# Seven block products in place of eight for the gate and up projections of sixteen experts in one decoder layer

## Chip, cores and metric

One core of a Trainium2 chip runs the whole layer as one program. The metric is the device time of one execution in microseconds (us); lower is better. The engines are PE (TensorE), DVE (VectorE), ACT (ScalarE), POOL (GpSimd) and SP (SyncE, which here only issues transfers). Each engine runs its own instruction list in order and waits on semaphores.

## What is computed

x is 8 x 512 tokens of width 512. Two attention parts add to it; then comes the feed-forward part, which the change touches:

```python
N, NK, C = 4096, 8192, 640                      # C = CAP: slots of an expert
probs = softmax(h @ router_w + router_b)        # h: normed tokens, 16 experts, top 2
expert_inputs[idx, pos] = h[token]              # (16, 640, 512)
y = (silu(e @ w_gate) * (e @ w_up)) @ w_down    # per expert, F = 704
out = x + shared_mlp(h) + sum over k of y[idx, pos] * weight
```

All inputs and outputs are fp32. A product of two fp32 matrices is made of three TensorE passes: each operand is split into a high part (rounded to fp32r by a copy) and a low part (the word minus its high part), and high*high, high*low and low*high are added in PSUM.

## The kernel before

Phase 1 (attention, router) runs batch by batch. Phase 2 has 24 groups: groups 0 to 7 are the shared MLP on the 8 batches of 512 tokens, groups 8 to 23 are the 16 experts, each on 640 gathered tokens (ET = 5 tiles of 128 tokens). F = 704 is cut into FC = 6 chunks of 128, the last of 64.

The weights of one job (shared, or one expert) are WC = 17 chunks of 128x512: gate and up for chunks 0 to 4 (ten), one "mixed" chunk with the last 64 columns of gate and of up, and six of down. Each goes from HBM to one of RAW = 6 raw buffers (SP, `load_weights`), then ACT copies its high part into a ring of 22 slots and POOL subtracts to get its low part (`split` on both engines, POOL's is L1426).

For one expert PE runs, for each of the five full chunks and each half of the tokens (`cuts`: 2 x 320 columns), gate and then up: four K chunks by three passes, so 5 x 2 x 2 x 12 = 240 matmuls of 320 columns, and 2 x 12 more for the mixed chunk (all in `three_pass`, L72). ACT makes silu of the gate (L1533), DVE multiplies it by up (L1599) into PSUM, ACT rounds the product (`h_hi`, L1491), DVE subtracts (`h_lo`, L1583). Then come the down products: five token tiles of 17 matmuls with 512 columns (L1692), which alternate between two PSUM banks. PE may start tile t only when DVE has scaled tile t-2 out of its bank:

```python
if n >= 2:
    pe.wait_ge(s_ost, n - 1)
```

Beside the down tiles the next expert's tokens are made ready. POOL has gathered them (L1439) at the start of this group, SP has turned them with DMA transposes into two 16-bit planes, ACT writes the upper halves of the words (`x_top`) and DVE the lower ones (`x_low`, L1567); ACT rounds (`x_hi`), DVE subtracts (`x_lo`, L1573). `tail` sets the order: work for token tile t, then the scaling of down tile t (L1636), which POOL adds to the output with an indirect DMA (L1480). L1491 is the line of the helper `copy`, so all ACT copies of phase 2 have it.

## Time and profile before

| what | value |
|---|---|
| time, median of 3 runs | 1820.36 us (1820.07 to 1820.89) |
| span of the profiled execution | 1818.3 us |
| PE busy | 1804.8 us, 99% |
| DVE, ACT, POOL busy | 873.3, 800.0, 922.2 us |
| one expert, start to start | 58.0 us |

The profiled execution's span is its own time as far as the profile shows it; it lies 2.1 us below the median of the runs. The kernel has 16 experts of equal work from 880.6 us to the end; the window of a whole expert taken below is 1112.58 to 1170.59 us, its gate and up until 1151.29 and its down tiles from there.

### The profile page before, as it was taken

To read this page: it belongs to the slowest core of one execution; us is meant where nothing else is said; L and a number is where in the kernel's file an instruction comes from. 1 tells how busy PE (TensorE), PEld (TensorE's weight loads), DVE (VectorE), ACT (ScalarE), POOL (GpSimd) and SP (SyncE) were. 2 spreads that over 40 slices of the span, in tenths; PEclk is the share of its full clock that TensorE was granted. 3 is DMA by queue.
4 is the path that set the end of the run, shared out by engine and by line. 5 is a ranking of instruction groups with operands and counts; after the bars stand their busy time and mean duration, and the time that the engine had idled before them with its cause. 6 is when DMAs were issued, how large, how long until landed. Compare 5 with 4: busy or idle time off the path is not lost.

```text
span 1818.3 us, 27202 instructions
## 1 busy us (share of the span) xinstructions
PE 1804.8 (99%) x9977; PEld 1598.7 (88%) x9977; DVE 873.3 (48%) x2067; ACT 800.0 (44%) x1574; POOL 922.2 (51%) x809
## 2 busy tenths in 40 slices
PE   9999999999999999999999999999999999999997
PEld 6888888888887878888999999999999999999997
DVE  6668777787745444332444324343334423443242
ACT  4555556555544343332444434444344434444331
POOL 3454464546653232225665656556665566656632
PEclk9999999999999999999999999999999999999999
DMA  8454555453552333225676676666666766667722
GB/s 319 147 134 122 151 140 150 134 143 95 147 116 40 47 52 68 37 42 103 161 141 132 163 156 134 135 150 158 147 140 126 164 149 140 145 138 163 145 41 29
DMA packets 254436, 229.35 MB, mean 126 GB/s; under 512 B 171712, under 2 KB 171968, under 8 KB 253024
## 3 DMA queue, kind: packets, MB, share of 16 engines
q1 hardware_dynamic: 228864, 174.51, 36.7%
q0 software_dynamic: 25440, 53.11, 17.3%
q8 instruction: 79, 1.29, 0.3%
q14 instruction: 53, 0.43, 0.1%
HBM read 138.80 MB, written 49.97 MB: 104 GB/s over the span
## 4 chain that ended last, share of the span: by engine, by line
PE 94%; DVE 2%; DMA 1%; issue 1%; POOL 1%; ACT 1%; SPq 0%; POOLq 0%; DVEq 0%; ACTq 0%
PE ps L72 66%; PE ps L1692 23%; PE ps L1002 3%; PE ps L1146 1%; PE ps L1008 0%; DMA buffer<-means 0%; ACT buffer L528 0%; DMA buffer<-in_x 0%; POOL buffer L481 0%; DMA means<-mean 0%; DVE buffer L832 0%; DVE stats L736 0%; DMA tokens_normed<-buffer 0%; ACT buffer L1491 0%; DMA buffer<-buffer 0%
## 5 line engine op out<-in xcount | busy, mean ns | idle before, releaser
L72 PE MATMUL ps<-buffer,buffer 128*128 128x320 f32 (+1 forms) x6900 | 1239.1, 341 | 1.3 <-DVE buffer L832 0.8
L72 PEld LDWEIGHTS ps<-buffer,buffer 128*128 128x128 f32 x6900 | 1121.0, 188 | 107.5 <-issue 1.5
L1426 POOL TENSOR_TENSOR buffer<-buffer,buffer 128x512 fp32r<-128x512 f32 x289 | 380.4, 1480 | 251.6 <-ACT buffer L1491 251.1
L1692 PE MATMUL ps<-buffer,buffer 128*128 128x512 f32 (+1 forms) x1921 | 437.6, 388 | 0.4 <-DVE buffer L1624 0.4
L1692 PEld LDWEIGHTS ps<-buffer,buffer 128*128 128x128 f32 x1921 | 356.9, 188 | 73.9 <-issue 1.2
L1533 ACT ACTIVATE buffer<-ps 128x320 f32<-128x320 f32 (+1 forms) x240 | 112.5, 469 | 599.6 <-PE ps L72 594.0
L1491 ACT ACTIVATE buffer<-buffer 128x512 fp32r<-128x512 f32 (+1 forms) x491 | 293.4, 652 | 163.4 <-PE ps L1692 90.6
L1599 DVE TENSOR_TENSOR ps<-ps,buffer 128x320 f32<-128x320 f32 (+2 forms) x198 | 100.2, 506 | 487.5 <-ACT buffer L1533 477.0
L1480 POOL DMA_INDIRECT out_tokens<-buffer,slot_list x79 | 124.0, 1569 | 185.5 <-DVE buffer L1636 177.3
L520 POOL DMA_INDIRECT slots<-pairs,slot_u x64 | 63.6, 994 | 181.8 <-DVE slot_u L989 164.8
L528 ACT ACTIVATE buffer<-buffer 128x512 fp32r<-128x512 f32 (+1 forms) x212 | 127.0, 683 | 19.9 <-DMA buffer<-buffer 15.2
L1636 DVE TENSOR_SCALAR buffer<-ps,slot_list 128x512 f32<-128x512 f32 (+1 forms) x81 | 60.1, 742 | 114.3 <-PE ps L1692 114.3
L533 ACT ACTIVATE buffer<-buffer,shift,rstd 128x512 f32<-128x512 f32 x96 | 70.5, 807 | 94.8 <-DVE shift L754 94.8
L1583 DVE TENSOR_TENSOR buffer<-ps,buffer 128x320 fp32r<-128x320 f32 (+2 forms) x198 | 96.7, 489 | 10.0 <-ACT buffer L1491 8.9
L1439 POOL DMA_INDIRECT buffer<-tokens_normed,slot_list x80 | 83.8, 1047 | 27.8 <-issue 27.8
L511 POOL TENSOR_TENSOR buffer<-buffer,buffer 128x512 f32<-128x512 f32 x32 | 40.5, 1293 | 103.1 <-DVE shift L754 99.1
L1491 ACT ACTIVATE buffer<-ps 128x320 fp32r<-128x320 f32 (+2 forms) x198 | 86.3, 436 | 0.7 <-DVE ps L1599 0.7
L528 ACT ACTIVATE buffer<-ps 128x512 fp32r<-128x512 f32 (+2 forms) x124 | 64.1, 557 | 43.9 <-PE ps L72 33.6
L1599 DVE TENSOR_TENSOR buffer<-ps,buffer 128x512 f32<-128x512 f32 (+1 forms) x42 | 29.0, 690 | 98.0 <-ACT buffer L1533 93.8
L1567 DVE COPY buffer<-buffer 128x512 uint16<-128x512 uint16 x80 | 72.0, 922 | 0.5
L736 DVE BATCH_NORM_STATS2 stats<-buffer 128x6 f32<-128x512 f32 x96 | 61.1, 682 | 7.8 <-DMA buffer<-in_x 7.7
L470 POOL TENSOR_TENSOR buffer<-buffer,buffer 128x512 fp32r<-128x512 f32 x28 | 38.4, 1405 | 37.3 <-ACT buffer L528 37.3
(134 smaller groups left out, 1094.0 us busy)
## 6 DMA issues: line engine op xcount, KB each, us to landing
buffer<-in_wts SPq DMA_DIRECT2D x289, 256.0 KB
buffer<-in_xT SPq DMA_DIRECT2D x8, 1024.0 KB, 5.5
buffer<-in_ctxT SPq DMA_DIRECT2D x8, 1024.0 KB, 8.2
out_tokens<-buffer SPq DMA_DIRECT2D x8, 1024.0 KB, 4.3
tokens_normed<-buffer SPq DMA_DIRECT2D x32, 256.0 KB, 3.1
out_tokens<-buffer POOLq DMA_DIRECT2D x32, 256.0 KB, 5.1
buffer<-in_x SPq DMA_DIRECT2D x7, 1024.0 KB, 5.5
buffer<-combiners_top SPq DMA_DIRECT2D x6, 1024.0 KB, 4.9
```

What stands on the lines that cost most here:

```text
L72: last = pe.matmul(out, left, right, start=(c == 0 and i == 0), stop=(c == len(parts) - 1 and i == 2))
L528: return act.activation(dst, src, ACT.Copy)
L533: act.activation(dst[:, t, :], x[b % XS][:, t, :], ACT.Identity, bias=shift[k][:, t:t + 1], scale=rstd[k][:, t:t + 1]).then_inc(done, 1)
L1426: pool.tensor_tensor(wl[n % RING][:], wraw[n % RAW][:], wh[n % RING][:].bitcast(F32), ALU.subtract).then_inc(s_wl, 1)
L1439: pool.indirect_dma_start(xn[:, t, :], None, Y[:, :], rows_at(groups[g][1], t), bounds_check=N + PAD - 1).then_inc(s_xg, 16)
L1480: pool.indirect_dma_start(out.rearrange("n (h d) -> (n h) d", h=parts), rows, ost[:, t, part_cols], None, bounds_check=parts * (N + PAD) - ...
L1491: return act.activation(dst, src, ACT.Copy)
L1533: act.activation(silu[u % TMP][0:rows_of(c), 0:n], bank[0:rows_of(c), 0:n], ACT.Silu)\
L1567: dve.tensor_copy(halves_of(t)[:, :, :, 0], xp[t][:, NC:2 * NC, :]).then_inc(s_xlow, 1)
L1583: dve.tensor_tensor(lo[:, first:first + n], product_of(u)[0:rows, 0:n], hh[0:rows, c, first:first + n].bitcast(F32), ALU.subtract).then_in ...
L1599: dve.tensor_tensor(product_of(u)[0:rows_of(c), 0:n], up_bank[u % 2][rows, 0:n], silu[u % TMP][0:rows_of(c), 0:n], ALU.mult).then_inc(s_ht, 1)
L1692: ins = pe.matmul(down_bank[(n + i) % 2][:, part_cols], left, right, start=(c == 0 and k == 0), stop=(c == FC - 1 and k == len(passes) - 1))
```

## The change

For experts only. A pair is the gate chunk and the up chunk of the same 128 features. Seen as a 2 x 2 block product (rows: gate and up; inner: two halves of K = 512; columns: two halves of the tokens, 64 of each tile of 128), it was eight block products. It becomes seven, by Winograd's form of Strassen's algorithm: three blocks of the weights and four sums of blocks (s1 to s4), against three blocks of the tokens and four sums of them (t1 to t4). A block product is 2 K chunks x 3 passes of 320 columns. The sums are made in fp32 on DVE and then split in high and low parts like all else (four slots for pairs, eight for single chunks; the ring is now the shared job's alone). The results need adding up after the product: two ACT copies out of PSUM (`kept`, `up1`) and five DVE additions (`pair_combined`); silu of the second half runs in SBUF. The high parts, sums and low parts of pair and single chunks are made at fixed places (`prepared`). POOL makes the low parts of all pairs in three instructions each (512, 256 and 1024 elements) and of four single chunks; DVE makes the other three (`BY_POOL = 4`). Both halves of the token words are now written by ACT. The gathered tokens (`xn`) share their place with `ost`.

The diff is cut to its core; plain renames and unchanged logic of the shared groups are left out.

```diff
-    RING = 22
     RAW = 6
     TMP = 3
-    TURN_AT = RAW + 4
+    PAIRS = FC - 1
+    SINGLES = WC - 2 * PAIRS
+    PAIR_SLOTS, SINGLE_SLOTS = 4, 8
+    PER_PAIR = 7
+    BY_POOL = 4
+    HALF, TH = CAP // 2, P // 2
+    TOKEN_PARTS = [(0, 2), (2, 4), (4, 5)]
...
+    prepared = {(3, 1): [("pair", 0)], (B - 1, 2): [("pair", 1)], (B - 1, 4): [("pair", 2)], (B - 1, "down0"): [("pair", 3)]}
+    for e in range(E):
+        q, m = e * PAIRS, e * SINGLES
+        prepared[B + e, 1] = [("pair", q + 4)]
+        prepared[B + e, 2] = [("single", m + i) for i in range(4)]
+        prepared[B + e, 3] = [("single", m + i) for i in range(4, SINGLES)]
+        if e + 1 < E:
+            prepared[B + e, 4] = [("pair", q + PAIRS)]
+            prepared[B + e, 5] = [("pair", q + PAIRS + 1)]
+            prepared[B + e, "down1"] = [("pair", q + PAIRS + 2)]
+            prepared[B + e, "down3"] = [("pair", q + PAIRS + 3)]
...
+        def low_parts(kind, i):
+            if kind == "single":
+                if i % SINGLES >= BY_POOL:
+                    return
+                n, k = single_chunk(i), single_slot(i)
+                pool.wait_ge(s_hi, parts_before_single(i) + 1)
+                pool.tensor_tensor(single_lo[k][:], wraw[n % RAW][:], single_hi[k][:].bitcast(F32),
+                                   ALU.subtract).then_inc(s_lo, 1)
+                return
+            n, k, done = pair_chunk(i), pair_slot(i), parts_before_pair(i)
+            hi, lo = pair_hi[k], pair_lo[k]
+            pool.wait_ge(s_hi, done + 1)
+            pool.tensor_tensor(lo[:, 0:2].rearrange("p b c f -> p (b c f)"), wraw[n % RAW][:],
+                               hi[:, 0:2].bitcast(F32).rearrange("p b c f -> p (b c f)"), ALU.subtract).then_inc(s_lo, 1)
+            pool.wait_ge(s_hi, done + 2)
+            pool.tensor_tensor(lo[:, 2].rearrange("p c f -> p (c f)"), wraw[(n + 1) % RAW][:, D // 2:D],
+                               hi[:, 2].bitcast(F32).rearrange("p c f -> p (c f)"), ALU.subtract).then_inc(s_lo, 1)
+            pool.wait_ge(s_hi, done + 3)
+            pool.tensor_tensor(lo[:, 3:7].rearrange("p b c f -> p (b c f)"),
+                               pair_sum[k][:].rearrange("p b c f -> p (b c f)"),
+                               hi[:, 3:7].bitcast(F32).rearrange("p b c f -> p (b c f)"), ALU.subtract).then_inc(s_lo, 1)
...
+        def high_parts(kind, i):
+            if kind == "single":
+                n = single_chunk(i)
+                loaded(act, n)
+                single_slot_free(act, i)
+                copy(single_hi[single_slot(i)][:], wraw[n % RAW][:]).then_inc(s_hi, 1)
+                return
+            n, hi = pair_chunk(i), pair_hi[pair_slot(i)]
+            loaded(act, n)
+            pair_slot_free(act, i)
+            copy(hi[:, 0:2].rearrange("p b c f -> p (b c f)"), wraw[n % RAW][:]).then_inc(s_hi, 1)
+            loaded(act, n + 1)
+            copy(hi[:, 2].rearrange("p c f -> p (c f)"), wraw[(n + 1) % RAW][:, D // 2:D]).then_inc(s_hi, 1)
+        def high_sums(kind, i):
+            if kind == "pair":
+                k = pair_slot(i)
+                act.wait_ge(s_sum, 4 * (i + 1))
+                copy(pair_hi[k][:, 3:7].rearrange("p b c f -> p (b c f)"),
+                     pair_sum[k][:].rearrange("p b c f -> p (b c f)")).then_inc(s_hi, 1)
+        def prepare(g, place, first=True, second=True):
+            for kind, i in prepared.get((g, place), []):
+                if first:
+                    high_parts(kind, i)
+                if second:
+                    high_sums(kind, i)
...
+        def words(e, t):
+            if t == 0:
+                act.wait_ge(s_xp, 16 * ET * (e + 1))
+                words_free(act, e)
+            copy(word_halves_of(t)[:, :, :, :, 1], turned_words(t, slice(0, NC))).then_inc(s_xraw, 1)
+            copy(word_halves_of(t)[:, :, :, :, 0], turned_words(t, slice(NC, 2 * NC))).then_inc(s_xraw, 1)
+        def token_hi(e, part):
+            cols = token_columns(part)
+            act.wait_ge(s_xraw, 2 * (ET * e + TOKEN_PARTS[part][1]))
+            if part == 0:
+                tokens_free(act, e)
+            copy(xh[:, :, :, cols], xw[:, :, :, cols]).then_inc(s_xh, 1)
+        def token_sum_hi(e, part):
+            n = len(TOKEN_PARTS) * e + part
+            cols = token_columns(part)
+            act.wait_ge(s_tsum, 4 * (n + 1))
+            act.wait_ge(s_xl, n + 1)
+            copy(th[:, :, :, cols], tw[:, :, :, cols]).then_inc(s_th, 1)
...
+        def pair_products(e, p):
+            g, q = B + e, e * PAIRS + p
+            u = unit_no[(g, p, 0)]
+            act.wait_ge(s_prod, PER_PAIR * q + 1)
+            if q > 0:
+                act.wait_ge(s_comb, 5 * (q - 1) + 2)
+            copy(kept[:], ps[0][:, 0:HALF]).then_inc(s_keep, 1)
+            if p > 0:
+                h_hi(e, p - 1, 0)
+                h_hi(e, p - 1, 1)
+            act.wait_ge(s_prod, PER_PAIR * q + 2)
+            if u - SHARED_UNITS >= 4:
+                act.wait_ge(s_hl, u - 2)
+            copy(up1[p % 2][:], cross_bank[p % 2][0][:, 0:HALF]).then_inc(s_keep, 1)
+            prepare(g, p, second=False)
+            act.wait_ge(s_prod, PER_PAIR * q + 4)
+            if q > 0:
+                act.wait_ge(s_ht, u - 1)
+            act.activation(silu0[:], ps[0][:, 0:HALF], ACT.Silu).then_inc(s_silu, 1)
+            prepare(g, p, first=False)
+            act.wait_ge(s_comb, 5 * q + 4)
+            act.activation(gate1[:], gate1[:], ACT.Silu).then_inc(s_silu, 1)
...
+            c = FC - 1
+            h_hi(e, c - 1, 0)
+            h_hi(e, c - 1, 1)
+            if e + 1 < E:
+                words(e + 1, 0)
+            for j, place in enumerate((silu0, gate1)):
+                act.wait_ge(s_mix, 2 * e + j + 1)
+                act.wait_ge(s_ht, unit_no[(g, c - 1, j)] + 1)
+                act.activation(place[0:FH, :], cross_bank[c % 2][j][0:FH, 0:HALF], ACT.Silu).then_inc(s_silu, 1)
+            for j in range(2):
+                h_hi(e, c, j)
+            prepare(g, c)
+            if e + 1 < E:
+                words(e + 1, 1)
+                token_hi(e + 1, 0)
+                words(e + 1, 2)
+                words(e + 1, 3)
+                token_hi(e + 1, 1)
+                token_sum_hi(e + 1, 0)
+                prepare(g, "down1")
+                words(e + 1, 4)
+                token_hi(e + 1, 2)
+                token_sum_hi(e + 1, 1)
+                token_sum_hi(e + 1, 2)
+                prepare(g, "down3")
...
+        def weight_sums(kind, i):
+            if kind == "single":
+                if i % SINGLES >= BY_POOL:
+                    n, k = single_chunk(i), single_slot(i)
+                    dve.wait_ge(s_hi, parts_before_single(i) + 1)
+                    dve.tensor_tensor(single_lo[k][:], wraw[n % RAW][:], single_hi[k][:].bitcast(F32),
+                                      ALU.subtract).then_inc(s_lo_dve, 1)
+                return
+            n = pair_chunk(i)
+            gate, up, sums = wraw[n % RAW], wraw[(n + 1) % RAW], pair_sum[pair_slot(i)]
+            s1, s2, s3, s4 = (sums[:, k].rearrange("p c f -> p (c f)") for k in range(4))
+            half = D // 2
+            loaded(dve, n)
+            loaded(dve, n + 1)
+            pair_slot_free(dve, i)
+            dve.tensor_tensor(s3, gate[:, 0:half], up[:, 0:half], ALU.subtract).then_inc(s_sum, 1)
+            dve.tensor_tensor(s1, up[:, 0:half], up[:, half:D], ALU.add).then_inc(s_sum, 1)
+            dve.wait_ge(s_sum, 4 * i + 1)
+            dve.tensor_tensor(s2, up[:, half:D], s3, ALU.subtract).then_inc(s_sum, 1)
+            dve.wait_ge(s_sum, 4 * i + 3)
+            dve.tensor_tensor(s4, gate[:, half:D], s2, ALU.subtract).then_inc(s_sum, 1)
...
+        def token_sums(e, part):
+            n = len(TOKEN_PARTS) * e + part
+            cols = token_columns(part)
+            b11, b21, b12, b22 = (xw[:, j, c:c + 2, cols] for j in range(2) for c in (0, 2))
+            t1, t2, t3, t4 = (tw[:, k, :, cols] for k in range(4))
+            dve.wait_ge(s_xraw, 2 * (ET * e + TOKEN_PARTS[part][1]))
+            if part == 0:
+                words_free(dve, e)
+            dve.tensor_tensor(t1, b12, b11, ALU.subtract).then_inc(s_tsum, 1)
+            dve.tensor_tensor(t3, b22, b12, ALU.subtract).then_inc(s_tsum, 1)
+            dve.wait_ge(s_tsum, 4 * n + 1)
+            dve.tensor_tensor(t2, b22, t1, ALU.subtract).then_inc(s_tsum, 1)
+            dve.wait_ge(s_tsum, 4 * n + 3)
+            dve.tensor_tensor(t4, b21, t2, ALU.subtract).then_inc(s_tsum, 1)
+        def token_lo(e, part):
+            cols = token_columns(part)
+            dve.wait_ge(s_xh, len(TOKEN_PARTS) * e + part + 1)
+            dve.tensor_tensor(xl[:, :, :, cols], xw[:, :, :, cols], xh[:, :, :, cols].bitcast(F32),
+                              ALU.subtract).then_inc(s_xl, 1)
+        def token_sum_lo(e, part):
+            cols = token_columns(part)
+            dve.wait_ge(s_th, len(TOKEN_PARTS) * e + part + 1)
+            dve.tensor_tensor(tl[:, :, :, cols], tw[:, :, :, cols], th[:, :, :, cols].bitcast(F32),
+                              ALU.subtract).then_inc(s_tl, 1)
...
+        def pair_combined(e, p):
+            g, q = B + e, e * PAIRS + p
+            u = unit_no[(g, p, 0)]
+            second, fourth = (bank[:, 0:HALF] for bank in cross_bank[p % 2])
+            up_1 = up1[p % 2][:]
+            if p > 0:
+                h_lo(e, p - 1, 0)
+                h_lo(e, p - 1, 1)
+            dve.wait_ge(s_prod, PER_PAIR * q + 3)
+            dve.wait_ge(s_keep, 2 * q + 2)
+            dve.tensor_tensor(up_1, fourth, up_1, ALU.add).then_inc(s_comb, 1)
+            prepare(g, p)
+            dve.wait_ge(s_prod, PER_PAIR * q + 5)
+            dve.wait_ge(s_comb, 5 * q)
+            dve.tensor_tensor(base[:], ps[1][:, 0:HALF], kept[:], ALU.add).then_inc(s_comb, 1)
+            dve.wait_ge(s_comb, 5 * q + 2)
+            dve.tensor_tensor(up_1, base[:], up_1, ALU.add).then_inc(s_comb, 1)
+            dve.wait_ge(s_prod, PER_PAIR * q + 6)
+            dve.wait_ge(s_ht, u)
+            dve.tensor_tensor(gate1[:], second, base[:], ALU.add).then_inc(s_comb, 1)
+            dve.wait_ge(s_prod, PER_PAIR * q + 7)
+            dve.wait_ge(s_hl, u)
+            dve.tensor_tensor(up0[:], fourth, base[:], ALU.add).then_inc(s_comb, 1)
+            dve.wait_ge(s_comb, 5 * q + 5)
+            dve.wait_ge(s_silu, u + 1)
+            dve.tensor_tensor(up0[:], up0[:], silu0[:], ALU.mult).then_inc(s_ht, 1)
+            dve.wait_ge(s_silu, u + 2)
+            dve.tensor_tensor(up_1, up_1, gate1[:], ALU.mult).then_inc(s_ht, 1)
...
+                pair_combined(e, p)
+            c = FC - 1
+            h_lo(e, c - 1, 0)
+            h_lo(e, c - 1, 1)
+            for j, (place, product) in enumerate(((silu0, up0), (gate1, up1[c % 2]))):
+                u = unit_no[(g, c, j)]
+                dve.wait_ge(s_silu, u + 1)
+                dve.wait_ge(s_hl, unit_no[(g, c - 1, 0)] + 1)
+                dve.tensor_tensor(product[0:FH, :], cross_bank[c % 2][j][FH:P, 0:HALF], place[0:FH, :],
+                                  ALU.mult).then_inc(s_ht, 1)
+            for j in range(2):
+                h_lo(e, c, j)
+            prepare(g, c)
+            if e + 1 == E:
+                for t in range(ET):
+                    scaled(g, t)
+                continue
+            token_sums(e + 1, 0)
+            token_lo(e + 1, 0)
+            scaled(g, 0)
+            token_sums(e + 1, 1)
+            token_lo(e + 1, 1)
+            token_sum_lo(e + 1, 0)
+            scaled(g, 1)
+            prepare(g, "down1")
+            token_sums(e + 1, 2)
+            token_lo(e + 1, 2)
+            scaled(g, 2)
+            token_sum_lo(e + 1, 1)
+            token_sum_lo(e + 1, 2)
+            prepare(g, "down3")
+            scaled(g, 3)
+            scaled(g, 4)
...
+        def product(bank, hi, lo, x_hi, x_lo, first):
+            for c in range(2):
+                passes = [(hi[:, c], x_hi[:, c]), (hi[:, c], x_lo[:, c]), (lo[:, c], x_hi[:, c])]
+                for i, (left, right) in enumerate(passes):
+                    ins = pe.matmul(bank[:, 0:HALF], left, right, start=(first and c == 0 and i == 0),
+                                    stop=(c == 1 and i == 2), skip_group_check=not first)
+            ins.then_inc(s_prod, 1)
+        def pair(e, p):
+            g, q = B + e, e * PAIRS + p
+            u = unit_no[(g, p, 0)]
+            wh_q, wl_q = pair_hi[pair_slot(q)], pair_lo[pair_slot(q)]
+            second, fourth = cross_bank[p % 2]
+            b11, b21, b22 = ((xh[:, j, c:c + 2], xl[:, j, c:c + 2]) for j, c in ((0, 0), (0, 2), (1, 2)))
+            t1, t2, t3, t4 = ((th[:, k], tl[:, k]) for k in range(4))
+            a11, a12, a22, s1, s2, s3, s4 = ((wh_q[:, k], wl_q[:, k]) for k in range(PER_PAIR))
+            pe.wait_ge(s_lo, low_parts_before_pair(q) + 3)
+            if p == 0:
+                pe.wait_ge(s_xl, len(TOKEN_PARTS) * (e + 1))
+            if q == 0:
+                pe.wait_ge(s_ht, SHARED_UNITS)
+            elif p == 0:
+                pe.wait_ge(s_silu, unit_no[(g - 1, PAIRS - 1, 0)] + 1)
+            else:
+                pe.wait_ge(s_silu, u - 1)
+            product(ps[0], *a11, *b11, True)
+            if p == 0:
+                pe.wait_ge(s_tl, len(TOKEN_PARTS) * (e + 1))
+            if p >= 2:
+                pe.wait_ge(s_comb, 5 * (q - 2) + 4)
+            elif p == 0 and e > 0:
+                pe.wait_ge(s_comb, 5 * (q - 1) + 4)
+            elif p == 1:
+                pe.wait_ge(s_hl, SHARED_UNITS)
+                if e > 0:
+                    pe.wait_ge(s_ht, unit_no[(g - 1, FC - 1, 0)] + 1)
+            product(second, *s1, *t1, True)
+            if p >= 2:
+                pe.wait_ge(s_comb, 5 * (q - 2) + 5)
+            elif p == 0 and e > 0:
+                pe.wait_ge(s_comb, 5 * (q - 1) + 5)
+            elif p == 1 and e > 0:
+                pe.wait_ge(s_ht, unit_no[(g - 1, FC - 1, 1)] + 1)
+            product(fourth, *s3, *t3, True)
+            pe.wait_ge(s_keep, 2 * q + 1)
+            product(ps[0], *a12, *b21, False)
+            if q > 0:
+                pe.wait_ge(s_comb, 5 * (q - 1) + 2)
+            product(ps[1], *s2, *t2, True)
+            pe.wait_ge(s_keep, 2 * q + 2)
+            product(second, *s4, *b22, False)
+            pe.wait_ge(s_comb, 5 * q + 1)
+            product(fourth, *a22, *t4, False)
```

## Rows read from the trace of the kernel before

**Rows 1.** Page, parts 1 and 4: busy time by engine, and the chain that ended last.

```profile
PE 1804.8 (99%) x9977; PEld 1598.7 (88%) x9977; DVE 873.3 (48%) x2067; ACT 800.0 (44%) x1574; POOL 922.2 (51%) x809
...
PE ps L72 66%; PE ps L1692 23%; PE ps L1002 3%; PE ps L1146 1%; PE ps L1008 0%; DMA buffer<-means 0%; ACT buffer L528 0%; DMA buffer<-in_x 0%; POOL buffer L481 0%; DMA means<-mean 0%; DVE buffer L832 0%; DVE stats L736 0%; DMA tokens_normed<-buffer 0%; ACT buffer L1491 0%; DMA buffer<-buffer 0%
```

**Rows 2.** The chain in order of time: start, us, what; one expert.

```profile
1112.58 38.72 PE ps L72 x264
1151.29 19.29 PE ps L1692 x85
```

**Rows 3.** Busy time of each engine in windows: gate/up and down of it.

```profile
1112.58:1151.29 38.71, 38.71 (x265) 38.71 (x265) 10.25 (x22) 15.45 (x35) 24.09 (x20) 1.00 0.73 163
1151.29:1170.59 19.30, 19.30 (x88) 15.96 (x87) 11.27 (x17) 9.14 (x16) 10.77 (x8) 1.00 0.60 110
```

**Rows 4.** Timeline of ACT in that expert: start, us, instruction, idle before.

```profile
1148.20 0.43 ACT L1491 ACTIVATE buffer<-ps 128x320 fp32r<-128x320 f32 x1
1148.52 1.15 ACT L1491 ACTIVATE buffer<-buffer 128x512 fp32r<-128x512 f32 x2
...
1153.40 1.93 ACT L1491 ACTIVATE buffer<-buffer 128x512 fp32r<-128x512 f32 x3
```

**Rows 5.** Groups of instructions by line and form: busy, mean ns of one.

```profile
L1491 ACT ACTIVATE buffer<-buffer 128x512 uint16<-128x512 uint16 x80 | 59.7, 774 | 0.0
...
L928 DVE TENSOR_TENSOR buffer<-ps,buffer 128x256 fp32r<-128x256 f32 x24 | 8.6, 417 | 2.7 <-ACT buffer L528 2.7
```

**Rows 6.** Timeline of DVE: two multiplications and roundings in a pair, then the down tiles.

```profile
1148.41 0.50 DVE L1599 TENSOR_TENSOR ps<-ps,buffer 128x320 f32<-128x320 f32 x1 [2.63 <-ACT buffer L1533]
1148.82 0.48 DVE L1583 TENSOR_TENSOR buffer<-ps,buffer 128x320 fp32r<-128x320 f32 x1
...
1158.55 0.67 DVE L1573 TENSOR_TENSOR buffer<-buffer,buffer 128x512 fp32r<-128x512 f32 x1
1159.14 0.75 DVE L1636 TENSOR_SCALAR buffer<-ps,slot_list 128x512 f32<-128x512 f32 x1
1159.80 0.45 DVE L1567 COPY buffer<-buffer 128x512 uint16<-128x512 uint16 x1
```

**Rows 7.** Timeline of POOL in that expert.

```profile
1115.31 8.12 POOL L1426 TENSOR_TENSOR buffer<-buffer,buffer 128x512 fp32r<-128x512 f32 x6
...
1129.01 1.03 POOL L1439 DMA_INDIRECT buffer<-tokens_normed,slot_list  x1 [0.30 <-issue]
1130.07 2.56 POOL L1426 TENSOR_TENSOR buffer<-buffer,buffer 128x512 fp32r<-128x512 f32 x2
...
1161.14 1.56 POOL L1480 DMA_INDIRECT out_tokens<-buffer,slot_list  x1 [0.30 <-issue]
```

**Rows 8.** Line L784, DVE subtractions with both inputs in SBUF: min/median/max ns.

```profile
L784 DVE TENSOR_TENSOR buffer<-buffer,buffer x12: 680/686/1728, 141.5 to 435.2; 128x512 fp32r<-128x512 f32 x12
```

**Rows 9.** Timeline of DVE and POOL where the longest of these ran.

```profile
435.24 1.73 DVE L784 TENSOR_TENSOR buffer<-buffer,buffer 128x512 fp32r<-128x512 f32 x1
...
435.14 1.29 POOL L470 TENSOR_TENSOR buffer<-buffer,buffer 128x512 fp32r<-128x512 f32 x1
...
436.38 1.74 POOL L470 TENSOR_TENSOR buffer<-buffer,buffer 128x512 fp32r<-128x512 f32 x1
```

**Rows 10.** Timeline of DVE and PE between shared group 7 and the first expert.

```profile
867.40 2.82 DVE L1567 COPY buffer<-buffer 128x512 uint16<-128x512 uint16 x2
870.99 0.90 DVE L1573 TENSOR_TENSOR buffer<-buffer,buffer 128x512 fp32r<-128x512 f32 x1 [0.76 <-ACT buffer L1491]
871.82 0.68 DVE L1624 COPY buffer<-ps 128x512 f32<-128x512 f32 x1
...
872.55 8.00 PE L1692 MATMUL ps<-buffer,buffer 128*128 128x512 f32 x34 [0.39 <-DVE buffer L1624]
```

**Rows 11.** Windows behind the last matmul; PEclk is the third number from the end.

```profile
1812.00:1818.30 6.30, 0.00 (x0) 0.00 (x0) 0.00 (x0) 0.00 (x0) 0.00 (x0) 0.59 0.19 21
```

538 lines of the change are left out of this document (306 added, 232 removed).

## The prediction

> **What bounds the kernel now.** I read the page first. PE is busy for 99% of the span, the other engines for half of it, and the chain that ended last lies on PE almost throughout [rows 1]. The chain in order of time then shows what an expert is: 264 matmuls of 320 columns in 38.72 us, 85 of 512 columns in 19.29 us, nothing between them, 58.01 us in all [rows 2]. So a gate/up matmul costs 38.72/264 = 0.147 us, and any matmul removed is time won, as long as the other engines keep up. They have room now: in the down window of 19.30 us DVE is busy for 11.27, ACT for 9.14, POOL for 10.77 us [rows 3].
>
> **What is removed.** A block product is 6 matmuls, 0.88 us. Five pairs lose one block product each: 30 matmuls, 4.40 us per expert, 70.4 us for 16. An unhindered expert takes 53.6 us: five pairs of 6.16, the mixed chunk 3.52, the down tiles 19.29.
>
> **What is added, and its price.** I price by start-to-start times in a run of one engine. ACT: 0.33 us for 320 columns, 1.15 - 0.63 = 0.52 for 512; for half words 1.93 - 0.52 - 0.77 = 0.64 [rows 4, 5]; at about 1 ns per element 256 are 0.26 and 1024 are 1.05. DVE: 0.41 for 320, 0.59 for 512 with both inputs in SBUF, 0.66 for a scaling [rows 6]; 256 columns last 417 ns, some 0.33 start to start [rows 5]; 1024 by the same slope 1.12. POOL: 1.28 for 512 (two in 2.56, six in 8.12), by size 0.64 and 2.56 for 256 and 1024, 1.03 + 0.30 to issue a gather, 1.6 to issue a scatter [rows 7].
>
> No row has 1024 elements on any of them. Such an operation costs no less than one of 512 and no more than two; I take near two, because from 320 to 512 columns ACT's price grows in proportion (0.33 to 0.52), so fixed cost is small. Were it one and a half, POOL's sum below would fall by 3.2 us, DVE's by 1.5 and ACT's by 2.4 per expert, and the time by some 15 x 3 = 45 us.
>
> Per expert this is:
> - ACT: five pairs of six 320-column operations (2.0) and 1.8 for high parts, mixed 1.3, single chunks 7 x 0.52, half words 10 x 0.64, tokens and their sums 2 x 2.6: about 36 us.
> - DVE: per pair nine 320-column operations (3.7) and four sums (1.3), mixed 1.6, three single chunks 1.8, token sums 3.3, two subtractions of 2560 elements 5.7, scalings 3.3: about 40 us.
> - POOL: 11,008 elements of subtraction, 27.5 us, and 15 us of gather and scatter issues.
>
> No engine exceeds 53.6 us by itself. Were that all, the forecast would be 1820 - 70 = 1750 us. Two things speak against it.
>
> **First: POOL and DVE exclude each other.** L784 is a DVE subtraction with both inputs in SBUF. Its median is 686 ns, its longest 1728 [rows 8]. That one started at 435.24, 0.10 us behind a POOL subtraction (435.14 to 436.43), and ended at 436.97, 0.54 us behind POOL's end; POOL's next one took 1.74 in place of 1.29 [rows 9]. Each waited for the whole instruction of the other. DVE operations that read PSUM show nothing of it. Before the change hardly any DVE operation of an expert has two SBUF inputs but the five of L1573. After it these have: the weight sums, `h_lo` (the product now lies in SBUF), one addition and both multiplications of a pair, three low parts, and everything on tokens, in all about 27 us. With POOL's 27.5 that is 55 us during which only one of the two may run, in an expert of 53.6. So even perfectly packed it is more than PE needs, and it isn't packed, since both wait on ACT and PE too.
>
> The Trainium skill ("GPSIMD Engine Reference", Specifications) has the two share their SBUF interfaces, with contention for VectorE instructions with two SBUF inputs; by that rule the 320- and 256-column ones count as well, which no row shows, and the trace agrees for 512. The same page (3.1) gives 4497 ns for a two-input operation of 2048 elements, 2.2 ns per element against 2.5 in my rows; by it POOL's part would be about 24 us and the sum of both 51, just under PE's.
>
> **Second: order beside the down tiles.** DVE now scales down tile 0 only behind `token_sums` and `token_lo` of part 0, and PE needs that scaling before tile 2; scaling 1 stands behind part 1, `token_sum_lo` and is needed before tile 3. All of that waits for ACT, which stands in `prepare` for DVE's weight sums. I walk through it with T = 0 at the end of pair 4, with 0.1 us for each hand-over, first without any collision:
> - mixed products end at 3.5, tile 0 runs 3.5 to 7.4, tile 1 to 11.2. `h_lo` of the mixed chunk ends at 5.9 and is in time (6.9).
> - DVE's weight sums end at 7.3; ACT, idle since 6.1, rounds them until 8.5, then `words` 1 to 9.9, `token_hi` 0 to 11.0.
> - `token_sums` 0 ends 11.6, `token_lo` 0 12.7, scaling 0 13.4: PE starts tile 2 at 13.5, 2.3 late.
> - words 2, 3 and `token_hi` 1 end at 15.0, `token_sum_hi` 0 at 16.1, `token_sum_lo` 0 17.8, scaling 1 18.5: tile 3 starts at 18.6.
> - ACT stands from 16.8 until the sums of "down1" at 20.0, rounds them to 21.1, `words` 4 to 22.5; `token_lo` 2 24.4, scaling 2 25.1: tile 4 runs 25.2 to 29.1.
>
> PE would be done at 22.8. The stall is 6.2 us against 4.4 saved: 59.9 us per expert, 1.8 more than before.
>
> Now with collisions, each booked as one whole POOL operation. In pair 2 POOL makes the low parts of pair 4 and then four single chunks, so DVE's additions alternate with operations of 1.28 and 2.56 us; PE waits about 3.2 us in pair 3, for `up1` on ACT and the first addition of DVE, and 0.3 in pair 4. At the end of pair 4 the 2.56 us operation for the next pair 0 stands before both multiplications, so they end at 6.2 and not 1.6; the mixed chunk's `h_lo` ends at 10.4, and tile 0 waits 3.6 us. Then scaling 0 ends at 20.9, scaling 1 at 25.2, scaling 2 at 33.4 (behind POOL's three operations of "down1"), and tile 4 at 37.4. The expert takes 30.8 + 3.5 + 37.4 = 71.6 us, 13.6 more than before. That is an upper value, for a collision costs less than a whole operation when POOL is already half through; I take off a quarter of the 11.7 us that collisions add: 68.7, or +10.7.
>
> A precedent stands in the trace: between group 7 and expert 0 five POOL subtractions meet DVE's copies; two copies of 0.45 us take 2.82, the first scaling comes at 871.82, and PE waits for it, 0.39 us [rows 6, 10].
>
> **Moved steps and new waits.** The lower half words go from DVE (five copies, 4 us with their waits, [rows 5, 6] have 0.34 for an undisturbed one) to ACT, already priced. The DMA transposes of the next tokens are issued by SP ahead of weight chunk 3 of the job after, that is, when single chunk 4 is released in pair 3; queued behind them are that pair's loads, needed by ACT some 12 us later. POOL's gather now waits for the scatters of the expert before; behind it stands pair 4's low part, which PE wants 24 us into the expert; gather and low part end by 19, so 5 us of cover. Scaling 0 also waits for the transposes, which come long before. All four I price at nothing; if the gather slipped by more than 5 us, pair 4 would wait for the rest.
>
> **Rest.** Fifteen experts have such an end. The last has none and saves 4.4. In group 7 the same chain on tokens, with all five tiles, stands beside only four down tiles (15.5 us): ACT has 13.5 us of work there and waits on DVE as above; I take 8 us (bounds 0 and 15). The four pairs prepared in the shared groups are hidden: ACT and DVE are half idle there [rows 1]; uncovered they cost some 2 us each. Loads are 17 chunks per expert as before; they are issued later, with raw buffers, but each has a pair's time to land; I price it at nothing, and at most 1 us per expert if single chunks 5 and 6 come late.
>
> Sum against the span: 1818.3 + 15 x 10.7 + 8 - 4.4 = 1982, and 2.1 us to the median (the table's span against its median): 1984 us, which I round to 1985.
>
> **Rivals.**
> - *Late, and blocked* (0.57): the walk above, 1920 to 2070.
> - *Late, hardly blocked* (0.23): POOL's operations fall where DVE reads PSUM or waits anyway. For it: 12 us of DVE's 40 aren't exclusive. Against: the two-input operations stand in rows of three or four. 59.9 to 64 us per expert: 1850 to 1920; for 60 us, 1852.
> - *Late, and PE slows* (0.10): PE would wait in stretches of 5 to 6 us. Behind its last matmul the granted clock falls to a mean of 0.59 within 6.3 us [rows 11], so to the lower level of 1.2 GHz for most of it; before, no wait of an expert lets it. If one down tile per expert ran at 1.2 GHz, it would take 3.86 us more, 15 x 3.9 = 58: above 2045. The Trainium skill ("TensorE: Matmul & The Clock Gate", What's actually happening) has an idle array throttled by default and released by activity; the trace agrees at the end of the program, and whether such short waits do it no row shows.
> - *Faster* (0.08): the stall stays under 4.4 us per expert. It hangs on one place, scalings 0 and 1 of DVE: they must be done by about 13 and 17 us behind T. That needs ACT to reach `token_hi` 1 some 2 us earlier, and POOL to stay out of the way. With no stall 1750, with half of it 1785.
> - *The stall equals the saving* (0.02): 1817 to 1824.
>
> **Range.** The cases from hardly blocked to blocked hold 0.80; the range runs from 1850 to 2070. A difference under 0.2% can't be told from no change here. Slower by more: 0.90; within: 0.02; faster: 0.08.
>
> **What would show it.** Right: 234 matmuls of 320 columns per expert; PE idle ahead of down matmuls, released by DVE's scaling; DVE's SBUF-only subtractions with medians far above their shortest, above all beside POOL; the chain leaving PE for ACT, DVE and POOL in each expert; start to start above 60 us. Wrong: PE without gaps at 53.6 us per expert; or DVE's operations at their shortest beside POOL's (then the exclusion is the failed step); or idle PE within the pairs and not beside the down tiles (then the walk's order is).

## The result, and the profile after

The changed kernel takes 2093.76 us (median of 4 runs, 2090.22 to 2096.11) against 1820.62 for the kernel before: 1.1501 times as long (1.1485 to 1.1517). The forecast was 1985 us, with a range up to 2070: the sign was right, the size was not.

The page of the changed kernel: engines with busy time and share, the chain that ended last, and the granted clock in 40 slices.

```profile
PE 1834.3 (88%) x9497; PEld 1591.9 (76%) x9497; DVE 1517.4 (72%) x2963; ACT 1019.8 (49%) x1910; POOL 1025.6 (49%) x841
...
PE 56%; DVE 25%; issue 11%; ACT 6%; DMA 1%; POOL 1%; DVEq 0%; SPq 0%; POOLq 0%; ACTq 0%
...
PEclk9999999999999999998898989989989989898999
```

PE has 480 matmuls fewer, as meant, and is busy for longer than before [rows 1], since part of them run at a lower clock (in `x_short_all` below, with the clock near 1.00, as many take 1741.1 us). A quarter of the chain now lies on DVE. POOL and the transfers hold 1% of it each, so work of POOL itself or late weights are hardly what PE waits for. The timeline of PE over one expert, which starts at 1120.37 (its first matmuls are left out) and whose successor starts at 1195.22 us (columns: start, duration, what, how many, and in brackets the idle time ahead and who ended it):

```profile
1129.75 11.93 PE L1970 MATMUL ps<-buffer,buffer 128*128 128x320 f32 x80
1146.94 12.28 PE L1970 MATMUL ps<-buffer,buffer 128*128 128x320 f32 x66 [5.27 <-ACT buffer L1605]
1159.06 3.68 PE L72 MATMUL ps<-buffer,buffer 128*128 128x320 f32 x24
1162.58 3.59 PE L2052 MATMUL ps<-buffer,buffer 128*128 128x512 f32 x15
1167.84 4.59 PE L2052 MATMUL ps<-buffer,buffer 128*128 128x512 f32 x19 [1.67 <-DVE buffer L1836]
1177.84 10.35 PE L2052 MATMUL ps<-buffer,buffer 128*128 128x512 f32 x34 [5.41 <-DVE buffer L1891]
1191.19 4.19 PE L2052 MATMUL ps<-buffer,buffer 128*128 128x512 f32 x17 [3.00 <-DVE buffer L1891]
1195.22 21.28 PE L1970 MATMUL ps<-buffer,buffer 128*128 128x320 f32 x144
```

L1970 is a block product, L72 the mixed chunk, L2052 a down product. PE waits four times: ahead of block product 4 of pair 3 (for ACT's `kept`, L1605), in down tile 0 (for `h_lo`, L1836), and ahead of tiles 2 and 4 (for DVE's scaling, L1891). From start to start the pairs take 38.7 us and the rest 36.2; over the 15 experts that have a successor the means are 39.1 and 36.8, and their start-to-start time is 75.85 on average, where it was 58.01.

In span: 15 x (75.85 - 58.01) = 267.6; the first expert starts 10.05 us later (890.43 against 880.39, where the text on the kernel before has 880.6); the last is 1.6 us shorter to PE's last matmul (56.75 against 58.38). Together 276.1, which is the difference of the spans, 2094.4 and 1818.3.

What holds DVE is seen best in the pairs. Here are ACT, DVE and POOL in pair 2 of the next expert:

```profile
1220.93 0.47 ACT L1695 ACTIVATE buffer<-buffer 128x320 f32<-128x320 f32 x1 [8.27 <-DVE buffer L1858]
1221.31 0.42 ACT L1605 ACTIVATE buffer<-ps 128x320 f32<-128x320 f32 x1
```

```profile
1212.59 0.47 DVE L1853 TENSOR_TENSOR buffer<-ps,buffer 128x320 f32<-128x320 f32 x1
1213.10 7.40 DVE L1855 TENSOR_TENSOR buffer<-buffer,buffer 128x320 f32<-128x320 f32 x1
1220.42 0.48 DVE L1858 TENSOR_TENSOR buffer<-ps,buffer 128x320 f32<-128x320 f32 x1
```

```profile
1212.83 2.40 POOL L1534 TENSOR_TENSOR buffer<-buffer,buffer 128x1024 fp32r<-128x1024 f32 x1
1215.20 4.95 POOL L1522 TENSOR_TENSOR buffer<-buffer,buffer 128x512 fp32r<-128x512 f32 x4
```

L1855 adds 320 columns, both inputs in SBUF. It started behind POOL's 1024-element subtraction and ended at 1220.50, 0.35 us behind the last of POOL's four single chunks (1220.15). Here it did not take its turn between two POOL instructions, it stood behind all five, and POOL's were not lengthened there (1.24 us each for the four, 1.28 in [rows 7]). ACT's silu waited 8.27 us for what follows it, `kept` stands behind that, and PE waited 5.28 us. Its neighbours L1853 and L1858 read PSUM and took 0.47 and 0.48 us. The lines over the whole run (minimum, median, maximum in ns):

```profile
L1853 DVE TENSOR_TENSOR buffer<-ps,buffer x80: 473/483/492, 898.4 to 2060.2; 128x320 f32<-128x320 f32 x80
L1855 DVE TENSOR_TENSOR buffer<-buffer,buffer x80: 491/493/7404, 898.9 to 2060.8; 128x320 f32<-128x320 f32 x80
L1836 DVE TENSOR_TENSOR buffer<-buffer,buffer x192: 477/488/8242, 901.8 to 2067.0; 128x320 fp32r<-128x320 f32 x160, 64x320 fp32r<-64x320 f32 x32
```

and in the groups by form, the same size with two SBUF inputs and with one in PSUM (after the bar busy us and mean ns):

```profile
L1855 DVE TENSOR_TENSOR buffer<-buffer,buffer 128x320 f32<-128x320 f32 x80 | 125.1, 1564 | 2.8
L1853 DVE TENSOR_TENSOR buffer<-ps,buffer 128x320 f32<-128x320 f32 x80 | 38.6, 483 | 20.5 <-PE ps L1970 20.5
```

Beside the down tiles the worst place is the first sum for the last token tile, on which the scaling for tile 4 waits in DVE's order:

```profile
1186.07 3.07 DVE L1803 TENSOR_TENSOR buffer<-buffer 128x128 f32<-128x128 f32 x1 [2.44 <-ACT buffer L1605]
```

```profile
L1803 DVE TENSOR_TENSOR buffer<-buffer 128x128 f32<-128x128 f32 x16 | 48.5, 3029 | 36.6 <-ACT buffer L1605 36.6
```

The Trainium skill ("GPSIMD Engine Reference", Specifications) tells of contention for VectorE's instructions with two SBUF inputs; the trace agrees at 320 columns, 1564 against 483 ns.

### The profile page after: what moved, and what is told of

It is laid out like the page before. It is cut to its first block, busy times and chain, and to the rows that moved or that the text cites. A ratio compares the mean times of both kernels' runs of the same rounds, so it can differ in the third digit from the quotient of the medians.

```text
span 2094.4 us, 27913 instructions
## 1 busy us (share of the span) xinstructions
PE 1834.3 (88%) x9497; PEld 1591.9 (76%) x9497; DVE 1517.4 (72%) x2963; ACT 1019.8 (49%) x1910; POOL 1025.6 (49%) x841
## 4 chain that ended last, share of the span: by engine, by line
PE 56%; DVE 25%; issue 11%; ACT 6%; DMA 1%; POOL 1%; DVEq 0%; SPq 0%; POOLq 0%; ACTq 0%
PE ps L72 27%; PE ps L1970 15%; PE ps L2052 10%; ACT buffer L1605 5%; DVE buffer L1803 4%; PE ps L1002 3%; DVE buffer L1864 2%; DVE buffer L1813 2%; DVE buffer L1784 2%; DVE buffer L1891 2%; DVE buffer L1836 1%; DVE buffer L1786 1%; DVE buffer L1853 1%; DVE buffer L1858 1%; DVE buffer L1861 1%
## 5 line engine op out<-in xcount | busy, mean ns | idle before, releaser
L72 PE MATMUL ps<-buffer,buffer 128*128 128x512 f32 (+1 forms) x3060 | 676.0, 380 | 1.3 <-DVE buffer L832 0.8
L1605 ACT ACTIVATE buffer<-buffer 128x512 fp32r<-128x512 f32 (+6 forms) x859 | 522.5, 666 | 309.8 <-DVE buffer L1788 199.9
L72 PEld LDWEIGHTS ps<-buffer,buffer 128*128 128x128 f32 x3060 | 557.1, 188 | 106.4 <-issue 1.5
L2052 PE MATMUL ps<-buffer,buffer 128*128 128x512 f32 (+1 forms) x1921 | 494.8, 418 | 156.5 <-DVE buffer L1891 127.9
L1970 PE MATMUL ps<-buffer,buffer 128*128 128x320 f32 x3360 | 537.5, 324 | 89.8 <-ACT buffer L1605 54.9
L1970 PEld LDWEIGHTS ps<-buffer,buffer 128*128 128x128 f32 x3360 | 529.0, 200 | 98.4 <-ACT buffer L1605 58.8
L2052 PEld LDWEIGHTS ps<-buffer,buffer 128*128 128x128 f32 x1921 | 385.3, 205 | 258.7 <-DVE buffer L1891 140.5
L1528 POOL TENSOR_TENSOR buffer<-buffer,buffer 128x512 fp32r<-128x512 f32 x80 | 125.1, 1564 | 269.1 <-ACT buffer L1605 268.8
L1534 POOL TENSOR_TENSOR buffer<-buffer,buffer 128x1024 fp32r<-128x1024 f32 x80 | 207.7, 2597 | 73.0 <-ACT buffer L1605 73.0
L1836 DVE TENSOR_TENSOR buffer<-buffer,buffer 128x320 fp32r<-128x320 f32 x192 | 137.2, 755 | 18.4 <-ACT buffer L1605 9.5
L528 ACT ACTIVATE buffer<-buffer 128x512 fp32r<-128x512 f32 (+1 forms) x212 | 126.8, 680 | 21.0 <-DMA buffer<-buffer 16.4
L1803 DVE TENSOR_TENSOR buffer<-buffer 128x256 f32<-128x256 f32 (+1 forms) x48 | 77.0, 1604 | 73.0 <-ACT buffer L1605 73.0
L1855 DVE TENSOR_TENSOR buffer<-buffer,buffer 128x320 f32<-128x320 f32 x80 | 125.1, 1564 | 2.8
L1605 ACT ACTIVATE buffer<-ps 128x320 f32<-128x320 f32 (+1 forms) x166 | 72.1, 435 | 56.0 <-PE ps L1970 55.2
```

The lines of the kernel that those rows point to most:

```text
L72: last = pe.matmul(out, left, right, start=(c == 0 and i == 0), stop=(c == len(parts) - 1 and i == 2))
L528: return act.activation(dst, src, ACT.Copy)
L1528: pool.tensor_tensor(lo[:, 0:2].rearrange("p b c f -> p (b c f)"), wraw[n % RAW][:], hi[:, 0:2].bitcast(F32).rearrange("p b c f -> p (b c ...
L1534: pool.tensor_tensor(lo[:, 3:7].rearrange("p b c f -> p (b c f)"), pair_sum[k][:].rearrange("p b c f -> p (b c f)"), hi[:, 3:7].bitcast(F3 ...
L1605: return act.activation(dst, src, ACT.Copy)
L1803: dve.tensor_tensor(t1, b12, b11, ALU.subtract).then_inc(s_tsum, 1)
```

## The experiments

All ratios are to the kernel before, measured beside each. Durations per expert are means over the same 15 starts. The theory: DVE is held by POOL, and `tail` has a late order on top. The rivals: the order alone, the clock alone, or DVE simply loaded with too much work.

### 1. POOL's subtractions cut to 32 columns

POOL makes only 32 columns of each low part of the experts' weights, and PE takes the high part in place of every one of these low parts, those that DVE makes too. So the kernel leaves out the low parts of the experts' weights; every instruction, matmul and wait stays, and DVE's work with them. The edit in short:

```diff
-pool.tensor_tensor(single_lo[k][:], wraw[n % RAW][:], single_hi[k][:].bitcast(F32), ...)
+pool.tensor_tensor(single_lo[k][:, 0:32], wraw[n % RAW][:, 0:32], single_hi[k][:, 0:32].bitcast(F32), ...)
...
-(lo[:, c], x_hi[:, c])
+(hi[:, c], x_hi[:, c])
```

> Leaves out: POOL computes only the first 32 columns of each low part of the expert weights, and PE uses the high part in its place; every instruction, semaphore and matmul stays. Exclusion theory (POOL's subtractions hold back DVE operations with two SBUF inputs): the DVE operations lose their long tails, an expert takes what the walk without collisions gave, 59.9 us, plus up to 3 us of slow clock: 1850 to 1900 us. Rival, DVE is simply loaded and chained too long: DVE's idle and PE's waits stay, over 2040 us.

Measured 1850.23 us, 1.0170 (1.0153 to 1.0187), 59.73 us per expert: pairs 31.0, rest 28.7. Timeline of PE beside the down tiles, and L1854, which is the addition L1855 of above:

```profile
1163.63 7.89 PE L2051 MATMUL ps<-buffer,buffer 128*128 128x512 f32 x34
1173.47 4.16 PE L2051 MATMUL ps<-buffer,buffer 128*128 128x512 f32 x17 [1.95 <-DVE buffer L1890]
1178.11 4.15 PE L2051 MATMUL ps<-buffer,buffer 128*128 128x512 f32 x17 [0.47 <-DVE buffer L1890]
1184.28 4.15 PE L2051 MATMUL ps<-buffer,buffer 128*128 128x512 f32 x17 [2.03 <-DVE buffer L1890]
```

```profile
L1854 DVE TENSOR_TENSOR buffer<-buffer,buffer x80: 491/492/601, 895.4 to 1812.4; 128x320 f32<-128x320 f32 x80
```

That is at the lower edge of what the exclusion theory expected, and far from the over 2040 us of a DVE that is simply loaded. No long additions are left, the wait ahead of block product 4 is gone, and the order alone costs about what the walk without collisions said: 59.9 us forecast, 59.73 measured. POOL's subtractions cost 75.85 - 59.73 = 16.1 us per expert, 15 x 16.1 = 242 of the 273 us.

### 2. The two causes one at a time, and together

`BY_POOL = 0` gives the four single chunks to DVE, so that no run of POOL subtractions follows the pair's:

```diff
-    BY_POOL = 4
+    BY_POOL = 0
```

> BY_POOL = 0: DVE makes all seven low parts of the single chunks, 2.4 us more work for it per expert, POOL 5.1 us less. Theory that DVE starves behind POOL instructions which follow one another without a gap (the 7.4 us of L1855 in each expert covers one of 1024 elements and four of 512): the wait of PE in pair 3 and the slow clock behind it go, 5 to 7 us per expert: 1990 to 2020 us. Theory that a DVE operation waits for one POOL operation only: 2070 to 2110. Load theory: 2.4 us more per expert, 2130.

`scaled` 0 to 3 go ahead of token work in DVE's `tail`:

```diff
+            scaled(g, 0)
             token_sums(e + 1, 0)
             token_lo(e + 1, 0)
-            scaled(g, 0)
+            scaled(g, 1)
             token_sums(e + 1, 1)
...
             prepare(g, "down1")
+            scaled(g, 2)
             token_sums(e + 1, 2)
...
+            scaled(g, 3)
             prepare(g, "down3")
-            scaled(g, 3)
```

> DVE scales down tiles 0, 1, 2 and 3 each ahead of the token work that it stood behind. If the order is what holds PE beside the down tiles, its 8.4 us of waits there go, but the tokens of the next expert are still ready only at about 1193 us of a down stage that PE now leaves earlier: it waits there in place. Gain 2 to 5 us per expert: 2020 to 2065. If the order doesn't matter (ACT and DVE chains set the pace alone): 2080 to 2095.

> BY_POOL = 0 and the scalings first, nothing left out. The two gains alone were 45 and 60 us. They concern different waits (pair 3, down tiles), so they should add: 1980 to 2000 us. If the second only moves a wait that the first has already moved: 2015 to 2035.

The last has both edits.

| kernel | us | ratio (interval) | per expert | pairs + rest |
|---|---|---|---|---|
| changed | 2093.76 | 1.1501 (1.1485 to 1.1517) | 75.85 | 39.1 + 36.8 |
| BY_POOL = 0 | 2048.51 | 1.1267 (1.1249 to 1.1286) | 72.81 | 35.3 + 37.5 |
| scalings first | 2034.03 | 1.1175 (1.1156 to 1.1193) | 71.88 | 39.9 + 32.0 |
| both | 1999.04 | 1.0981 (1.0963 to 1.0999) | 69.52 | 37.5 + 32.0 |

The order is worth 4 us, won behind the pairs (36.8 to 32.0) with 0.8 given back in them. The four single chunks on POOL are worth 3 us, won in the pairs (39.1 to 35.3), and the longest stalls get shorter:

```profile
L1855 DVE TENSOR_TENSOR buffer<-buffer,buffer x80: 491/492/1995, 897.8 to 2012.4; 128x320 f32<-128x320 f32 x80
L1836 DVE TENSOR_TENSOR buffer<-buffer,buffer x192: 477/487/5158, 900.8 to 2018.7; 128x320 fp32r<-128x320 f32 x160, 64x320 fp32r<-64x320 f32 x32
```

The expectations for the scalings first and for both together came true. That for `BY_POOL = 0` did not: 2048.51 us lies between what starving behind a run gives (1990 to 2020) and what waiting for one operation gives (2070 to 2110). DVE now has 2.4 us more work per expert, and a stall of 5.16 us is left; how the missing gain divides between the two is not shown.

### 3. The order mended where POOL is short

`x_short_first` is the edit of `x_pool_short` with the scalings first. `x_short_all` also puts ACT's token words ahead of its wait for the weight sums, here and in the same way at "down1":

```diff
-            prepare(g, c)
+            prepare(g, c, second=False)
             if e + 1 < E:
                 words(e + 1, 1)
+                prepare(g, c, first=False)
                 token_hi(e + 1, 0)
```

> Both together: POOL's low parts cut to 32 columns with PE using the high part in their place (leaves out the low parts of the expert weights), and DVE scales the down tiles first. If the collisions and the order are all that held the experts, PE's waits beside the down tiles (5.6 us per expert without collisions) go and an expert takes 53.6 to 55 us: 1755 to 1790 us. If the last tokens of the next expert are late instead (ACT and DVE need 22 us for them anyhow), only part is won: 1810 to 1840.

> POOL's low parts cut to 32 columns with PE using the high part in their place (leaves out the low parts of the expert weights), the scalings first, and ACT's words before its wait. Without collisions an expert took 56.6 us with the scalings first, of which 3.7 us waits: if these are ACT being late in pair 0 behind its work of down3, this order wins 0.5 to 2 us each: 1775 to 1797. If not, 1800 to 1808.

Measured 1804.97 us, 0.9916 (0.9899 to 0.9932), and 1764.21 us, 0.9700 (0.9684 to 0.9717), with 54.19 us per expert, in most of them 53.9. The first falls between its two expectations, the second is faster than its range: the words ahead of the wait win 2.6 us per expert and not 0.5 to 2. From the last pairs to the end of the down tiles PE runs without a gap in `x_short_all`:

```profile
1158.89 31.26 PE L1971 MATMUL ps<-buffer,buffer 128*128 128x320 f32 x210
1189.99 3.68 PE L72 MATMUL ps<-buffer,buffer 128*128 128x320 f32 x24
1193.51 18.77 PE L2053 MATMUL ps<-buffer,buffer 128*128 128x512 f32 x82
```

So the seven block products save 4.1 of their 4.4 us per expert, and ACT and the transfers keep up. With both orders mended, only what POOL and DVE do to each other stands between the change and a gain. But both kernels leave out the low parts of the experts' weights, so neither is a way to have it.

### 4. Is it the clock?

Behind a long wait PE is slow: over 1145 to 1150 and 1175 to 1180 us the granted clock of the changed kernel has means of 0.53 and 0.61 (the windows, with the busy time of PE, its weight loads, DVE, ACT and POOL, then clock, DMA share and GB/s):

```profile
1145.00:1150.00 5.00, 3.06 (x11) 3.06 (x12) 4.83 (x11) 3.78 (x9) 0.31 (x1) 0.53 1.12 200
1175.00:1180.00 5.00, 2.16 (x5) 1.78 (x6) 4.90 (x10) 4.76 (x8) 1.28 (x1) 0.61 0.02 3
```

The 34 down matmuls behind the second wait take 10.35 us against 7.89 in `x_pool_short`; the 66 of pair 3 take 12.28, where 66 x 0.147 = 9.7. To see what that costs, matmuls with no use are put in the waits:

```diff
+                if t in (2, 4) and e + 1 < E:
+                    pe.wait_ge(s_silu, unit_no[(g, PAIRS - 1, 0)] + 1)
+                    for _ in range(34 if t == 2 else 18):
+                        pe.matmul(ps[0][:, 0:HALF], single_hi[single_slot(m + 1)][:, 0:P], hh[:, 0, 0:HALF],
+                                  start=True, stop=True)
```

and in the same way in pair 3, 24 ahead of block product 6 in the first kernel (with 24 ahead of tile 2), 34 ahead of block product 4 in the second.

> Adds 24 matmuls of 320 columns without use (3.5 us) in each of PE's two longest waits of an expert: in pair 3 ahead of the wait for the second kept copy, and ahead of down tile 2. Clock theory: the granted clock stays at 1.0, and the 66 gate/up matmuls and 34 down matmuls behind these waits take 9.7 and 7.7 us and not 12.3 and 10.35: up to 5.2 us per expert, 2015 to 2040. If the clock falls anyhow or costs nothing: 2085 to 2100 (the added ones are hidden in waits of over 5 us).

> As the added matmuls before, but placed ahead of the block product that really waits in pair 3 (the fourth, for the first kept copy): 34 there (5.0 us of a wait of 5.3), 34 ahead of down tile 2 (5.0 of 5.4), 18 ahead of tile 4 (2.6 of 3.0). Clock theory: no stretch below 1.0, the 66 and 34 matmuls behind the waits are back at 9.7 and 7.7 us; 3 to 5 us per expert won: 2020 to 2050. If the waits aren't covered by it: over 2094.

Measured 2163.85 us, 1.1899 (1.1879 to 1.1919), and 2154.35 us, 1.1837 (1.1817 to 1.1856). Neither shows the gain of the clock theory. In the pairs both miss: the first has its matmuls behind the wait instead of in it, and in the second the wait moved to pair 2, so they come on top. One down part of the second tells more (PE's timeline, and the window over it; L2100 are the added ones):

```profile
1262.02 4.57 PE L2056 MATMUL ps<-buffer,buffer 128*128 128x512 f32 x19 [1.67 <-DVE buffer L1836]
1266.43 5.14 PE L2100 MATMUL ps<-buffer,buffer 128*128 128x320 f32 x34
1272.08 4.16 PE L2056 MATMUL ps<-buffer,buffer 128*128 128x512 f32 x17 [0.50 <-DVE buffer L1891]
1276.47 4.17 PE L2056 MATMUL ps<-buffer,buffer 128*128 128x512 f32 x17 [0.23 <-DVE buffer L1891]
...
1285.47 4.15 PE L2056 MATMUL ps<-buffer,buffer 128*128 128x512 f32 x17 [2.20 <-DVE buffer L1891]
1289.45 5.73 PE L1970 MATMUL ps<-buffer,buffer 128*128 128x320 f32 x38
```

```profile
1257.00:1289.40 32.40, 27.80 (x137) 23.22 (x136) 25.77 (x42) 19.49 (x31) 14.19 (x10) 1.00 0.28 52
```

The clock is 1.00 and tiles 2 and 3 take 4.16 us each, yet from the first down matmul (1256.76) to the next expert (1289.45) it is 32.7 us, as in the changed kernel (1162.58 to 1195.22, 32.6, mean clock 0.90):

```profile
1162.58:1195.22 32.64, 22.56 (x88) 17.45 (x87) 25.92 (x42) 19.52 (x31) 14.36 (x10) 0.90 0.28 51
```

Here a faster PE only waits longer for the scalings, and none of the 15 down parts of `x_warm2` is shorter than 32.6 us. So slow matmuls in tiles 2 and 3, ahead of another wait, cost nothing. Tile 4 is another matter, for behind it the next expert starts at once. One of `x_pool_short`, with the window over it:

```profile
1004.17 5.76 PE L2051 MATMUL ps<-buffer,buffer 128*128 128x512 f32 x17 [2.02 <-DVE buffer L1890]
```

```profile
1004.30:1010.00 5.70, 5.70 (x19) 4.53 (x20) 3.64 (x7) 1.77 (x3) 2.88 (x3) 0.70 0.41 57
```

This tile takes 5.76 us in place of 4.15, and its expert 60.56 in place of 58.95. It happens in 5 of 15 experts there, and in 4 of 15 of the changed kernel: in the mean 0.4 us per expert (1.6 x 4/15). In the pairs the slow clock can cost from 0 to 12.28 - 9.7 = 2.6 us per expert, which stays open.

### 5. Why does DVE stand behind a whole run?

If a waiting DVE instruction went in at the next boundary between two POOL instructions, cutting the 1024-element one in two would help:

```diff
-            pool.tensor_tensor(lo[:, 3:7]..., pair_sum[k][:]..., hi[:, 3:7]..., ALU.subtract).then_inc(s_lo, 1)
+            for first in (3, 5):
+                last = pool.tensor_tensor(lo[:, first:first + 2]..., pair_sum[k][:, first - 3:first - 1]..., ...)
+            last.then_inc(s_lo, 1)
```

> POOL's subtraction of 1024 elements is made in two of 512. If a waiting DVE operation gets in between any two POOL instructions, it waits 1.3 us where it waited 2.5, and 2 to 4 us per expert are won: 2030 to 2065. If it can starve behind a run of POOL instructions, cutting them changes little: 2085 to 2105.

Measured 2131.49 us, 1.1697 (1.1677 to 1.1717), 78.28 per expert: worse than either expectation. DVE and POOL in the same place:

```profile
1216.73 8.37 DVE L1839 TENSOR_TENSOR buffer<-buffer,buffer 128x320 fp32r<-128x320 f32 x1
```

```profile
1217.37 2.50 POOL L1535 TENSOR_TENSOR buffer<-buffer,buffer 128x512 fp32r<-128x512 f32 x2
1219.84 4.91 POOL L1522 TENSOR_TENSOR buffer<-buffer,buffer 128x512 fp32r<-128x512 f32 x4
```

DVE ended at 1225.10, 0.35 us behind the last of these (1224.75). Here the run is one block for DVE, though it is cut finer. That is no rule for every run. In the changed kernel, in the expert from 1120.37, DVE had its turn between two POOL instructions that follow each other directly; it ended at 1157.64, with the second of them under way:

```profile
1156.15 1.49 DVE L1783 TENSOR_TENSOR buffer<-buffer,buffer 128x256 f32<-128x256 f32 x1
```

```profile
1156.06 1.30 POOL L1528 TENSOR_TENSOR buffer<-buffer,buffer 128x512 fp32r<-128x512 f32 x1 [10.75 <-ACT buffer L1605]
1157.32 0.93 POOL L1531 TENSOR_TENSOR buffer<-buffer,buffer 128x256 fp32r<-128x256 f32 x1
```

Counted over the experts of the changed kernel's trace, a DVE instruction with SBUF inputs alone outlasted five or six POOL subtractions 14 times (once in each of 14 experts), two or three 15 times, and one 130 times. To keep DVE out of the long run, the run itself is broken, with one wait that holds POOL's first single chunk until DVE has ended pair 2:

```diff
                 n, k = single_chunk(i), single_slot(i)
+                if i % SINGLES == 0:
+                    pool.wait_ge(s_ht, unit_no[(B + i // SINGLES, 2, 1)] + 1)
                 pool.wait_ge(s_hi, parts_before_single(i) + 1)
```

> The changed kernel with one wait more: ahead of its first single chunk POOL waits until DVE has multiplied the second half of pair 2. Starvation theory: the run behind which DVE stood for 7.4 us ends with the operation of 1024 elements, so the longest DVE operation of the pairs falls to about 2.3 us and PE's wait of 5.3 us in pair 3 nearly goes: 75 us won if the slow clock behind it costs nothing, up to 115 us if it costs its 2.6 us in full: 1980 to 2020. One-operation theory: DVE got its turn anyhow and the added wait only makes POOL later: 2085 to 2110.

Measured 2075.84 us, 1.1399 (1.1380 to 1.1418), 74.79 per expert, between the two expectations. The addition now waits for one POOL instruction at most:

```profile
L1857 DVE TENSOR_TENSOR buffer<-buffer,buffer x80: 491/492/2482, 896.5 to 2042.3; 128x320 f32<-128x320 f32 x80
```

And POOL's four single chunks, still without a gap between them, now take turns with DVE:

```profile
1137.57 5.99 POOL L1524 TENSOR_TENSOR buffer<-buffer,buffer 128x512 fp32r<-128x512 f32 x4 [4.71 <-DVE buffer L1868]
```

```profile
1138.39 2.32 DVE L1838 TENSOR_TENSOR buffer<-buffer,buffer 128x320 fp32r<-128x320 f32 x2 [0.90 <-ACT buffer L1607]
```

They last 5.99 us where they lasted 4.95. So what makes DVE stand behind a run is neither its length nor the lack of a gap alone; the runs do not show what it is.

The pairs fell from 39.1 to 35.9 us, the rest rose from 36.8 to 38.9: the four subtractions now come later and meet the work behind the pairs. The 5.3 us wait is gone, and shorter waits stand in its place (in one expert 2.12, 0.38 and 0.86 us in the pairs).

### 6. The way back, as far as it goes

With POOL's subtractions at full size: both edits of 2 with ACT's words first (`x_combo2`); both edits of 2 with two of DVE's results put in PSUM, so that fewer of its instructions have two SBUF inputs (`x_psum`); all of them (`x_all`); and with `BY_POOL = 4` and the wait of 5 (`x_all_gap`).

```diff
+            sum_1 = in_bank[1][:, 0:HALF] if p % 2 == 0 else up_1
+            up_0 = in_bank[0][:, 0:HALF]
...
-            dve.tensor_tensor(up_1, base[:], up_1, ALU.add).then_inc(s_comb, 1)
+            dve.tensor_tensor(sum_1, sum_1, base[:], ALU.add).then_inc(s_comb, 1)
```

> On top of BY_POOL = 0 and the scalings first (1999 us): ACT writes token words before, and not behind, its wait for DVE's weight sums at the mixed chunk and at down1. If ACT's blocking in its own order is a part of the late tokens, 1 to 2 us per expert: 1970 to 1990. If DVE alone sets the pace of that chain: 1995 to 2005.

> On top of BY_POOL = 0 and the scalings first (1999 us): the products and sums of a pair (up0 always, up1 of even pairs) lie in the two PSUM banks that the down tiles don't need meanwhile, so 19 of the 25 exclusive 320-column DVE operations of the pairs have only one input in SBUF; nothing is left out, PE waits for the last rounding of pair 4 before down tile 0. Exclusion theory: these 19 run beside POOL, the PE wait in pair 3 (3.5 us) and part of that in pair 0 go: 1930 to 1970 us. If DVE is merely loaded, no change: 1990 to 2010.

> The two before together, with BY_POOL = 0 and the scalings first. If both gains are real and lie in different places (pairs, down tiles) they add: 1910 to 1950. It beats the kernel before only if an expert comes under 58 us, which these gains don't reach.

> The scalings first, ACT's words first, products in PSUM, and POOL's hand-over, with BY_POOL back at 4. Against BY_POOL = 0 (1960 us) DVE has 2.4 us less per expert and POOL 5.1 us more of exclusive time, of which one run meets pair 3: 1935 to 1975. If the exclusive time of POOL as such decides and not when it comes, it is slower than 1960 by 2 us per expert: 1990.

| kernel | us | ratio (interval) | per expert |
|---|---|---|---|
| x_combo2 | 1994.42 | 1.0960 (1.0942 to 1.0978) | 69.13 |
| x_psum | 1965.69 | 1.0813 (1.0793 to 1.0833) | 67.14 |
| x_all | 1960.39 | 1.0780 (1.0762 to 1.0798) | 67.05 |
| x_all_gap | 1939.05 | 1.0659 (1.0641 to 1.0677) | 65.46 |

With fewer instructions that have two SBUF inputs, 69.52 - 67.14 = 2.4 us per expert are won, as the exclusion theory expected; a merely loaded DVE would have given 1990 to 2010 us. The words first bring hardly anything while DVE and POOL are in each other's way: `x_combo2` and `x_all` are slower than hoped for (1970 to 1990, 1910 to 1950). `x_all_gap` is in its range, and 1.6 us per expert faster than `x_all` although POOL has four more subtractions: POOL's exclusive time as such does not decide. None comes near the 57.5 us per expert (58.01 less a fifteenth of the 10.05 - 1.6 at the two ends, an estimate) at which the change would break even; of the kernels with POOL's subtractions at full size, the one before remains the fastest.

## Why the prediction was wrong

**Right.** The sign. The saving (4.40 us per expert): 53.9 us in most experts of `x_short_all` against an ideal of 53.6. The order: the walk without collisions gave 59.9, `x_pool_short` 59.73. That they agree so closely is in part luck: most of its experts take 58.95, with waits of 1.95, 0.47 and 2.03 us at tiles 2, 3 and 4 where the walk had 2.3, 1.2 and 2.7, and five with a slow tile 4 and a first one of 62.48 raise the mean. Exclusion of POOL and DVE as the main cost, and that instructions which read PSUM are spared. Between group 7 and expert 0: 8 us forecast, 10.05 measured. A little off: the last expert gained 1.6 us and not 4.4, for its pairs collide too (its DVE and POOL work in the pairs is the same) and take some 33.6 us, not 30.8.

**The step that failed** is the size of the collisions: "each booked as one whole POOL operation", and "I take off a quarter of the 11.7 us that collisions add". They add 16.1 us (75.85 - 59.73), where I booked 11.7 and took 8.8. Split by place: behind the pairs the full booking gave 37.4 us, and 36.8 were measured, so the quarter that I took off had no ground there. In the pairs it gave 30.8 + 3.5 = 34.3, and 39.1 were measured: a wait of 5.3 us in pair 3 where I had "about 3.2", since DVE's addition stood behind five POOL instructions and did not "alternate" with them, and up to 2.6 us of slow matmuls behind it. So of the 7.15 us per expert that the forecast lacks, some 4.8 lie in the pairs and 2.3 to 2.4 in the quarter. The precedent of the kernel before could not warn of it: its two copies of 0.45 us that took 2.82 [rows 6, 10] took 1.38 and 1.55, each behind one POOL instruction (so a copy with one SBUF input can be held too). The sum of 30.8, 3.5 and 37.4 is 71.7 and not 71.6, which changes nothing. In the sum: 75.85 - 68.7 = 7.15 us per expert, 107 us; with 2 us more at the start and 2.8 less gained at the end that is 112, the difference of the span (2094.4) from the 1982 of the sum.

**A sign that came in part.** I expected DVE's SBUF-only subtractions to have medians far above their shortest. Beside the down tiles one does: the 128x128 sums of L1803 take 3029 ns in the mean, and the shortest of that line 284. In the pairs none does: the median of L1836 is 488 ns, its shortest 477. Most run unhindered there, and a few long stalls make the cost.

**The rivals.** "Hardly blocked" and "faster" fall with the result, and experiment 1 shows what they lack. "Late, and PE slows", at 0.10, had its sign seen rightly: the clock does fall behind waits of 5 us. But its price, one slow down tile per expert at 3.9 us, is not paid: experiment 4 shows slow matmuls in tiles 2 and 3 hidden by the next wait, and a slow tile 4, 1.6 us longer, in 4 of 15 experts. The time is in its range, for the most part for another reason.

**Open.** When a DVE instruction gets its turn behind one POOL instruction and when it stands behind a run is not settled: in the changed kernel the median of L1836 is 488 ns and its longest 8242. Also open is the share of the slow clock in the pairs, 0 to 2.6 us per expert.

## What to carry to other kernels

Where work is moved to DVE, count its instructions with two SBUF inputs, and add their time to POOL's. Here the sum was 55 us in a stage of 53.6, and a saving of 4.4 us per expert became a loss of 17.8, though no engine's own load exceeded the stage. When the two meet counts for more than the sum: look for the places where a DVE instruction that PE waits for falls into a run of POOL instructions, and book the rest of that run there, with nothing taken off. Put one operand in PSUM where that can be. Cutting POOL's instruction did not help here. And before a slow clock is blamed, look whether another wait follows the slow matmuls: only where none does is their time lost.

## What the runs showed of the hardware

- A DVE instruction with two SBUF inputs of 320 columns took 0.49 us alone and 7.40 us beside a run of POOL subtractions; 8.37 us behind an even longer one. POOL's instructions kept their 1.24 us there for 512 elements and 2.40 for 1024. With one input in PSUM the same size took 0.47 to 0.49 us throughout.
- DVE can also get its turn between two POOL instructions that follow directly (1.49 us for 256 columns, where 0.41 is the shortest).
- POOL's 1024-element subtraction takes near two of 512 (2.40 against 1.24 us), as the forecast took it.
- Around waits of 5.3 and 5.4 us the granted clock had means of 0.53 and 0.61, so it stood at 1.2 GHz for most of those windows, and the matmuls behind were slower by a quarter to a third. Behind the waits of 2 us ahead of tile 4 of `x_pool_short` the tile took 4.15 us in ten experts and 5.76 in five, where the clock had a mean of 0.70.
